# AdaLN-conditioned mixture-of-LoRA FFN: x's transposes and Bx regrouped over the tiles, the router's steps moved, Bx spread in fp32r

## The reference, cut to what matters

```python
# x (8, 512, 2048); cond_A, cond_B: 8 adapters of rank 16; base_w (2048, 2048), base_b (2048,)
# ffn A (64, 2048), ffn B (16 experts, 2048, 64), router_w (16, 2048)
def cond(x, A, B, ids):                      # one adapter per batch
    Bx = einsum('bni,bri->bnr', x, B[ids])
    return einsum('bnr,bor->bno', Bx, A[ids])
def ffn(y):
    base = einsum('bsi,oi->bso', y, base_w) + base_b
    hid = einsum('bsi,ri->bsr', y, A)
    probs = softmax(einsum('bsi,ei->bse', y, router_w))
    topw, topi = top_k(probs, 2);  topw /= sum(topw) + 1e-6
    combine = sum(one_hot(topi, 16) * topw)  # (b, s, 16)
    return base + 0.5 * einsum('bse,bsr,eor->bso', combine, hid, B)
out = x + ffn(cond(x, cond_A, cond_B, ids))
```

## Time and profile before

| | us |
|---|---|
| median of 3 runs (lowest, highest) | 446.38 (445.77, 449.51) |
| the profiled execution, its own time | 445.62 |
| its span, first to last instruction | 443.8 |
| PE busy in it | 409.7 (92%) |
| DVE busy | 319.4 (72%) |
| ACT busy | 108.1 (24%) |
| POOL busy | 40.5 (9%) |

### The profile page before, as it was taken

How to read it: one execution, slowest core, us unless ns; L and a number is a source line. 1 busy time by engine, 2 the same in 40 slices (tenths; PEclk the granted TensorE clock), 3 DMA queues, 4 the chain that set the end, 5 groups by cost and what they waited for, 6 DMA issues and landing times.

```text
span 443.8 us, 6785 instructions
## 1 busy us (share of the span) xinstructions
PE 409.7 (92%) x2496; PEld 279.9 (63%) x2496; DVE 319.4 (72%) x830; ACT 108.1 (24%) x163; POOL 40.5 (9%) x53
## 2 busy tenths in 40 slices
PE   0597997999788999999999999999999999999996
PEld 0475985656556766666667666666666676666665
DVE  2699996999468496668677875966686778756453
ACT  0003114435473231123113112311231131123110
POOL 4020000002100120012001201200120012012000
PEclk9999998999999999999999999999999999999999
DMA  8999999999999999899999999998999898556935
GB/s 223 357 330 331 334 357 366 345 269 336 289 295 239 352 362 323 279 349 342 310 287 378 306 315 302 366 312 295 348 335 325 285 366 303 207 201 217 343 128 189
DMA packets 75027, 135.35 MB, mean 305 GB/s; under 512 B 5506, under 2 KB 14770, under 8 KB 74994
## 3 DMA queue, kind: packets, MB, share of 16 engines
q1 hardware_dynamic: 56000, 102.08, 69.7%
q10 hardware_dynamic: 18994, 32.84, 23.5%
HBM read 99.23 MB, written 35.65 MB: 304 GB/s over the span
## 4 chain that ended last, share of the span: by engine, by line
PE 63%; DVE 10%; DMA 9%; SPq 6%; POOL 3%; ACT 3%; issue 3%; ACTq 2%; POOLq 0%; DVEq 0%
PE ps L927 13%; PE ps L928 11%; PE ps L929 11%; PE ps L901 11%; PE ps L941 6%; DMA bexpT<-in_x 6%; PE ps L930 5%; POOL u_r L480 3%; DMA gm_r<-xT 3%; DVE xT L728 3%; DVE early L659 3%; SPq L296 3%; ACT bexpT L495 2%; PE ps L856 2%; PE ps L949 2%
## 5 line engine op out<-in xcount | busy, mean ns | idle before, releaser
L840 DVE TENSOR_TENSOR xbuf<-ps,xbuf 128x512 f32<-128x512 f32 x128 | 86.7, 677 | 96.0 <-PE ps L930 96.0
L927 PE MATMUL ps<-h_r,u_r 128*128 128x512 f32 x256 | 108.8, 425 | 0.7
L928 PE MATMUL ps<-h_r,u_r 128*128 128x512 f32 x256 | 100.3, 392 | 0.0
L929 PE MATMUL ps<-h_r,u_r 128*128 128x512 f32 x256 | 100.1, 391 | 0.0
L866 PE MATMUL ps<-early 128*128 128x256 f32 x256 | 66.5, 408 | 22.6 <-DVE early L659 22.6
L728 DVE STREAM_TRANSPOSE xT<-xbuf 128x256 f32<-128x256 f32 x224 | 80.6, 410 | 0.0
L866 PEld LDWEIGHTS ps<-early 128*128 128x128 f32 x256 | 48.1, 201 | 36.8 <-issue 16.5
L927 PEld LDWEIGHTS ps<-h_r,u_r 128*128 128x128 f32 x256 | 48.1, 188 | 35.9 <-issue 16.7
L659 DVE STREAM_TRANSPOSE early<-xbuf 128x256 f32<-128x256 f32 x128 | 65.9, 577 | 5.3 <-issue 3.8
L901 PE MATMUL ps<-bexpT,cur 128*32 128x512 f32 x512 | 61.6, 598 | 2.2 <-DVE h_r L707 1.5
L495 ACT ACTIVATE h_r<-ps 128x512 fp32r<-128x512 f32 x64 | 36.2, 595 | 78.8 <-PE ps L901 78.4
(11 more groups left out here) (67 smaller groups left out, 205.3 us busy)
## 6 DMA issues: line engine op xcount, KB each, us to landing
out<-xbuf SPq DMA_DIRECT2D x31, 1024.0 KB, 7.3
xbuf<-in_x SPq DMA_DIRECT2D x28, 1024.0 KB, 7.4
xbuf<-in_x ACTq DMA_DIRECT2D x32, 512.0 KB, 10.9
xbuf<-in_x SPq DMA_DIRECT2D x32, 512.0 KB, 8.6
xbuf<-in_L_ffn_base_w SPq DMA_DIRECT2D x16, 512.0 KB, 19.3
xbuf<-in_L_ffn_base_w ACTq DMA_DIRECT2D x16, 512.0 KB, 20.1
gm_r<-g_hilo SPq DMA_DIRECT2D x128, 32.0 KB, 6.8
early_u<-in_L_ffn_B SPq DMA_DIRECT2D x10, 256.0 KB, 18.5
```

The costliest lines, as they stand in the source:

```text
L840: dve.tensor_tensor(xs, ps[:, tile_bank(b.n, m), :], xs, ALU.add).then_inc(s_out, 1)
L927: pe.matmul(acc, u_r[:, b.q, 0, h, tok_t], hi, start=(h == 0), stop=False)
L928: pe.matmul(acc, u_r[:, b.q, 0, h, tok_t], lo, start=False, stop=False)
L929: pe.matmul(acc, u_r[:, b.q, 1, h, tok_t], hi, start=False, stop=False)
```

## The change

x's transposes for a batch are now two per tile over 16 tiles, begun at tile 4 of two batches before and ended at tile 3 of the batch before (batches 0 and 1 have a schedule of their own). They stand behind the slot. Bx is computed in three groups (11, 11 and 10 products), each behind an h chunk: at tile 12 of the batch two before, and at tiles 0 and 4 of the batch before. The router's steps move: logits from 9 to 7, top 2 from 10 to 8, comb from 11 to 9, combk from 12 to 10, both flips from 13 and 14 to 11, u to 11. Batch 0 (for fronts 0 and 1) keeps its places except that the spread comes one slot after the logits and both flips are at 13. Bx is copied out once more in fp32r (`bxs_r`, high part by ACT, low part by DVE), and the spread is two fp32r products. The router's small tiles have their own memory, for which the DMA scratch is set to 1024 bytes. Refills of x move from tiles 4 and 8 (ACT) and chunks 0 and 1 (SP) to tiles 4 and 12.

```diff
-        spread = sb("spread", [P, 2, P])
+        spread = sb("spread", [P, 2, P], F32R)
+        bxs_r = sb("bxs_r", [P, 2, T], F32R)
+        router = sb("router", [P, 4, T])
-        sel = xT[:, 0, 0:NT * 2 * E]...       # comb, wt2, topf, topi, combk likewise
+        sel = router[:, 0, 0:NT * 2 * E]...
-        T_FIRST = {m: (2 * m, 2 * m + 1) for m in range(8)}
-        T_AHEAD = {12: (0,), 13: (1,), 14: (2,), 15: (3, 4)}
-        T_AT = {0: (5, 6), 1: (7,), 3: (8, 9), 4: (10, 11), 5: (12,), 6: (13, 14), 7: (15,)}
-        REFILL_AT = {4: 0, 8: 1}
-        def bx_before(f, m):
-            return {4 if f.n == 1 else 3: range(0, KD), 8: range(KD, 2 * KD)}.get(m, ())
+        LATE_AT = MT // 4
+        X_GROUPS = (11, 22)
+        def x_transposes(b, m):
+            if b == 0:
+                n, at = (1, 4 * m) if m < 8 else (2, 4 * (m - 10))
+                return [(n, at + i) for i in range(4) if 0 <= at < 2 * KD // n]
+            if b == 1 and m < 6:
+                return [(2, k) for k in range(KD + (0, 3, 6, 9, 12, 14)[m], KD + (3, 6, 9, 12, 14, 16)[m])]
+            if b == 1:
+                per, at = (2, 2 * (m - 6)) if m < 12 else (3, 12 + 3 * (m - 12))
+                return [(3, k) for k in range(at, at + per)]
+            if m < LATE_AT:
+                return [(b + 1, 2 * KD - 2 * LATE_AT + 2 * m + i) for i in range(2)]
+            return [(b + 2, 2 * (m - LATE_AT) + i) for i in range(2)]
+        def bx_groups(b, m):
+            a, e = X_GROUPS
+            if b == 0:
+                groups = {4: (1, (0, KD)), 8: (1, (KD, 2 * KD))}
+            elif b == 1:
+                groups = {0: (2, (0, KD)), 6: (2, (KD, 2 * KD)), 12: (3, (0, a))}
+            else:
+                groups = {0: (b + 1, (a, e)), 4: (b + 1, (e, 2 * KD)), 12: (b + 2, (0, a))}
+            return [groups[m]] if m in groups else []
+        def refills(b, m):
+            if b == 0:
+                return {4: [(2, 0)], 8: [(2, 1)]}.get(m, [])
+            if b == 1:
+                return {0: [(3, 0)], 8: [(3, 1)]}.get(m, [])
+            return {0: [(4, 0)] if b == 2 else [], 4: [(b + 2, 1)], 12: [(b + 3, 0)]}.get(m, [])
-        BXP_AT = 8
-        SPREAD_AT, MAX_AT, EXP_AT, TOP_AT, COMB_AT, COMBK_AT = 9, 9, 9, 10, 11, 12
-        CT_AT = UP_AT = {13: 0, 14: 1}
+        Steps = namedtuple("Steps", "bxp bx_lo logits peak exp spread top comb comb_k flips u")
+        FIRST_STEPS = Steps(8, 9, 9, 9, 9, 10, 10, 11, 12, 13, {13: (0,), 14: (1,)})
+        SECOND_STEPS = Steps(6, 6, 7, 7, 7, 7, 8, 9, 10, 11, {11: (0, 1)})
+        LATER_STEPS = Steps(4, 5, 7, 7, 7, 7, 8, 9, 10, 11, {11: (0, 1)})
...
 # ACT, slot: after the copy of Bx
+                    need(act, s_rep, f.n)
+                    copy(bxs_r[:, 0, :], ps[:, BXB, :]).then_inc(s_bxhi, 1)
 # DVE, slot
+                if m == at.bx_lo:
+                    dve.wait_ge(s_bxp, f.n + 1)
+                    dve.wait_ge(s_bxhi, f.n + 1)
+                    dve.tensor_tensor(bxs_r[:, 1, :], bxp, f32(bxs_r[:, 0, :]), ALU.subtract).then_inc(s_bxlo, 1)
 # DVE, step: the slot is behind the addition at every tile, and the transposes behind the slot
-                        if f is not None and m < MT - 1:
+                        if f is not None:
                             slot(f, m)
-                        if b.n + 2 < NB:
-                            for j in T_AHEAD.get(m, ()):
-                                x_transpose(Batch(b.n + 2), 2 * j)
-                                x_transpose(Batch(b.n + 2), 2 * j + 1)
+                        for n, k in present(x_transposes(b.n, m)):
+                            x_transpose(Batch(n), k)
 # PE, slot
-                    pe.matmul(ps[:, BXB, :], spread[:, f.q, :], bxp,
-                              start=True, stop=True).then_inc(s_rep, 1)
+                if m == at.spread:
+                    pe.wait_ge(s_bxhi, f.n + 1)
+                    pe.wait_ge(s_bxlo, f.n + 1)
+                    pe.matmul(ps[:, BXB, :], spread[:, f.q, :], bxs_r[:, 0, :], start=True, stop=False)
+                    pe.matmul(ps[:, BXB, :], spread[:, f.q, :], bxs_r[:, 1, :], start=False, stop=True)\
+                      .then_inc(s_rep, 1)
-                if m in CT_AT:
-                    h = CT_AT[m]
+                if m == at.flips:
                     pe.wait_ge(s_combk, f.n * 2 + 2)
+                    for h in range(2):                # both halves; half 1 waits for s_bx
...
+                        for n, span in present(bx_groups(b.n, c * NT + t)):
+                            bx_products(Batch(n), span)
                         tile_products(b, c, t)
...
-    nc = bacc.Bacc("TRN2", target_bir_lowering=False, num_devices=1)
+    nc = bacc.Bacc("TRN2", target_bir_lowering=False, num_devices=1, dynamic_dma_scratch_size=1024)
```

More of the change, by code:

```diff
@@ L23 @@
+from collections import namedtuple
 from contextlib import ExitStack
@@ L407, in step @@
                         continue
-                    if f is not None and c < 2 and not is_last(f):
-                        xquad_free(sp, f, c)
-                        load_xquad(sp, f.n + 1, c, range(0, NQ // 2))
+                    for n, g in present(refills(b.n, c * NT)):
+                        xquad_free(sp, n, g)
+                        load_xquad(sp, n, g, range(0, NQ // 2))
                     sp.wait_ge(s_out, b.n * MT + NT * (c + 1))
@@ L540, in h_hi, with slot @@
                     copy(h_r[:, c % 2, 0, h, :], ps[:, HB + h, :]).then_inc(s_hhi, 1)
[L542 to L546, removed]
+            def slot(f, m):
+                at = steps_of(f)
+                if m == at.bxp:
                     act.wait_ge(s_bxq, (f.n + 1) * 2 * KD)
@@ L591, in _ @@
                 if n in SLOT_AT:
-                    if SLOT_AT[n] in UP_AT:
+                    if SLOT_AT[n] in FIRST_STEPS.u:
                         act.wait_ge(s_gst[2], 16)
-                    slot(first, SLOT_AT[n], False)
+                    slot(first, SLOT_AT[n])
             act.wait_ge(s_wmm, NW)
@@ L610, in step @@
                             copy_experts(E_LATE[c * NT + t])
+                        for n, g in present(refills(b.n, c * NT + t)):
+                            xquad_free(act, n, g)
+                            load_xquad(act, n, g, range(NQ // 2, NQ))
                         if f is not None:
@@ L711, in x_transpose @@
                 g, j = k // KD, k % KD
-                place = ring_place(f, j)
                 cols = slice(j * SQ, (j + 1) * SQ)
@@ L722, in x_transpose, with slot @@
                         dve.wait_ge(s_xquad[g], f.n * NQ * 16)
-                if g == 0 and place == 0:
-                    need(dve, s_ct, f.n * 2)
                 if f.n < 2 and g == 0 and j in (KD // 2, 3 * KD // 4):
                     dve.wait_ge(s_ef, [e for e in range(GROUPS) if E_SLOT[e] == j // 4 + 1][f.n] + 1)
-                need(dve, s_bxq, f.n * 2 * KD + (0 if f.n == 2 and g == 0 else k - KD + 1))
-                dve.transpose(xh[:, place, :].rearrange("p (t l) -> p t l", l=SQ), src).then_inc(s_xe, 1)
-            def slot(f, m, x_too=True):
+                need(dve, s_bxq, f.n * 2 * KD + k - KD + 1)
+                dve.transpose(xh[:, j, :].rearrange("p (t l) -> p t l", l=SQ), src).then_inc(s_xe, 1)
+            def slot(f, m):
                 base = f.n * DVE_PER_FRONT
-                at = {MAX_AT: 0, TOP_AT: 1, COMB_AT: 10}.get(m, 0)
-                count = [at]
+                at = steps_of(f)
+                count = [{at.top: 1, at.comb: 10}.get(m, 0)]
                 def link(ins):
@@ L743, in wide @@
                     return ap.unsqueeze(2).to_broadcast([P, NT, E])
[L745 to L748, removed]
+                if m == at.bx_lo:
+                    dve.wait_ge(s_bxp, f.n + 1)
+                    dve.wait_ge(s_bxhi, f.n + 1)
+                    dve.tensor_tensor(bxs_r[:, 1, :], bxp, f32(bxs_r[:, 0, :]), ALU.subtract).then_inc(s_bxlo, 1)
+                if m == at.peak:
                     dve.wait_ge(s_lg, f.n + 1)
@@ L773, in slot @@
                                                   op0=ALU.add, op1=ALU.add))
-                if m == COMB_AT:
+                if m == at.comb:
                     after()
@@ L818, in _ @@
                 if n - SLOT_LAG in SLOT_AT:
-                    slot(first, SLOT_AT[n - SLOT_LAG], False)
+                    slot(first, SLOT_AT[n - SLOT_LAG])
             h_lo(first, 0)
@@ L931, in tile_products, with bx_products @@
                   .then_inc(s_acc, 1)
-            def bx_products(f, m):
-                for k in bx_before(f, m):
+            def bx_products(f, span):
+                for k in range(*span):
                     g, j = k // KD, k % KD
@@ L941, in bx_products @@
                     pe.matmul(ps[at:at + BK, BXB, g * (T // 2):(g + 1) * (T // 2)], bT[:, j, f.half, :],
-                              xh[:, ring_place(f, j), :], start=(j < NQ), stop=(j >= KD - NQ)).then_inc(s_bxq, 1)
```

(4 more changed lines are left out.)

55 lines of the change are left out of this document (26 added, 29 removed).

## The result

The changed kernel takes 482.86 us in the median (480.66 to 489.99), against 445.65 us for the kernel before measured beside it (445.35 to 449.51). The ratio is 1.080, 95% interval 1.075 to 1.085: 37 us slower. The forecast was 462, with a range of 453 to 469: the direction is right, but it gave 16 of the 37 us, and the measured time lies above the range. The profiled execution took 482.72, its span is 480.6.

The account below looks back on a forecast made before the run. PE was taken as the bound from the second batch on. Waits 18.4, less savings 7.9, plus first front 0.5, gave +11.0; clock falls +5.1; 445.62 became 461.7, put at 462 because the runs' median lay 0.8 higher. Range 453 to 469.

Parts of the forecast that it names:

- What bounds the kernel: From the second batch on, nothing is paid except through PE, busy 40.55 of a batch's 40.65 us.
- The savings, 1.3 a batch: PE work and waits removed in batches 2 to 5: 0.52 + 0.38 + 0.2 + 0.18 us; 7.9 in all batches.
- the group: Tile 3's Bx products, moved behind h chunks, take 1.72 us where they took 2.24: 0.52 saved a batch.
- the spread: Bx spread in the tiles' fp32r format: logits and spread save 0.38 us of PE a batch.
- the flips: Both flips of comb at one place, before an h chunk, take 0.78 us where they took 1.0: about 0.2 saved.
- the third cut of Bx: Cutting Bx into a third group costs nothing, as every group continues fp32 work.
- The wait at the flips: Behind tile 11, PE waits for comb: 3.1 us in batches 1 to 5, 2.4 in batch 6; none in batch 0.
- u sooner: PE's wait for the low half of u at the h chunk ending a batch goes: 0.18 us saved.
- The clock: Behind the new waits the clock falls to 1.2 GHz, 1.7 us each; 3 of 6 taken, +5.1 us.
- falls each time: Rival: the clock falls behind all six new waits, 10.2 us, total 468; chance 0.17.
- Part 7: Refills of x are asked for 8 tiles, about 19 us, ahead of the first transpose; nothing taken for them.
- x comes late: Rival: transposes wait for x, PE waits for Bx; 5 us in a few batches, total 470 to 480; chance 0.05.

Follow-up runs that it names:

- e8: Kernel before with the fp32r spread, the first Bx group behind an h chunk and both flips at tile 13, router and x unmoved: 439.89 us, ratio 0.986.
- e7: Kernel before with only Bx spread as two fp32r products one tile behind the logits, and the small DMA scratch: 444.33 us, ratio 0.996.
- the two doses: e4 and e5, which shorten DVE's chain to comb by 0.69 and 1.86 us against e1: 468.94 and 465.55 us.
- e5: e1 with no x transposes at tiles 8 to 10 and chunk 2's h halves made at tile 8, ahead of its result: 465.55 us, ratio 1.046.
- e10: e9 with all refills of x issued by ACT and none by SP: 453.82 us, ratio 1.017.
- e1: Changed kernel with batch 4's first-half refill of x issued at the end of batch 1: 475.05 us, ratio 1.063.
- e2: e1 with 12 unread products of 512 columns on PE ahead of the flips in fronts 2 to 7: 461.57 to 469.81 us, ratio 1.041.
- e4: e1 with x's two transposes of tile 8 done at tile 7: 468.94 us, ratio 1.053.
- e9: e5 with the flips behind tile 12's h chunk, the Bx group at tile 13 and batch 3's refill issued early: 461.34 us, ratio 1.034.
- e11: Changed kernel with ACT issuing all four quadrants of each refill of x and SP none: 471.94 us, ratio 1.056.

## Why the prediction was right or wrong, point by point

1. **What bounds the kernel**: right. Every gain and loss that was traced went through PE.
2. **The savings, 1.3 a batch**: a little high. e8 measures 40.65 - 39.61 = 1.04 a batch: about 0.49 for the group, 0.34 for the spread (e7), 0.17 for u, and only 0.06 for the flips, where 0.2 was counted. In the changed kernel one saving is eaten further: the third cut of Bx is not free, tile 3 to 4 takes 4.96 where 3.68 + 1.08 = 4.76 was counted.
3. **The wait at the flips, 3.1 in batches 1 to 5 and 2.4 in batch 6**: right in its place and its cause, which the two doses show. As idle time in the records it was to be 2.9; it is 2.94, 2.96 and 2.94 in batches 2 to 4, 3.77 in batch 1, 3.27 in batch 5, and 2.29 in batch 6.
4. **u sooner, and batch 0**: the wait for u at the start of a batch is gone, but in batch 1 a Bx group now stands at tile 0 and waits 0.76 for batch 0's u, which I had not looked for. The group at tile 6 of batch 1 waits for its last transposes too: tile 5 to 6 takes 4.74, where 1.59 + 2.25 = 3.84 was counted.
5. **The clock: a term that was mis-sized.** I took 3 falls of 6 at 1.7 each, 5.1. There were 5. With the wait taken off, tile 11 to 12 is 1.4 to 1.7 us longer in batches 1 to 4 than in e5 at full clock (6.0), and 2.9 longer in batch 5, where the clock stayed low for twice as long: 9.0 in all. The 3 of 6 was a choice between two bounds and no count. The case "falls each time" stood beside it with 0.17. The Trainium skill (TensorE: Matmul & The Clock Gate, section HAM oscillation) describes waits repeated in a loop that drop the clock each time. The trace agrees for batches 1 to 5, and not for batch 6.
6. **The refills: the step that failed.** Part 7 said that each quadrant group is asked for 8 tiles ahead, and took nothing for it. The diff has exceptions in plain sight: `{0: [(4, 0)] if b == 2 ...}` asks for batch 4's first half 4 tiles ahead, and batch 3's halves are asked for 6 and 5 tiles ahead. And SP reaches the refill for batch 4 8.7 us after the batch's first tile starts (225.2, against 216.5), since it stands at a reload until a store has landed; the data then takes 14.5 to land, 239.7 against a need at 228.8. With the lags that the prediction itself names, SP some 4 behind and a landing of 9.3 or at most 20.7, the same four tiles give 216.5 + 4 + 9.3 = 229.8 or 241, a wait of 1 to 12 us: not the 11, but a likely loss. The rival "x comes late" had the mechanism with 5 us at a chance of 0.05, and in its place it named the Bx groups at tile 12 or 4, where it was the spread at tile 7. "With a longer batch DMA gets easier" was wrong as well. From 150 to 400 us, first the kernel before, then the changed one, the DMA engines are busier and carry less, and SP's quadrants land after 14.6 us in the median in place of 8.6:

```profile
150.00:400.00 250.00, 249.28 (x1584) 162.85 (x1587) 182.59 (x524) 54.56 (x99) 25.50 (x25) 1.00 0.93 314
150.00:400.00 250.00, 223.53 (x1372) 145.55 (x1371) 166.26 (x476) 50.72 (x94) 23.85 (x24) 0.94 1.01 285
```

The sum: 11.0 of waits and savings as forecast, then from measured pieces 9.0 for the clock behind the flips, 11.0 for x in batch 2 (9.3 of wait and 1.6 of half clock behind it), 0.8 for the longer wait of batch 1 (DVE had waited 2.6 for x there), 0.9 and 0.8 for the two Bx groups of batch 1, 1.0 for tile 4's groups: 34.5 of the 36.8 between the last tiles' ends (476.86 against 440.09). Some 2 us are not assigned; the savings that came out lower, 0.3 a batch, are probably among them.

Still open: why the DMA engines are busier with fewer bytes in the changed order of transfers. That a batch is longer explains the lower GB/s (293 over batch 3 of the changed kernel, 332 over a batch of e8, nearly the same bytes), but not that the busy share is as high (1.01 and 1.00). The edits on SP's queue relieved the lateness but did not end it in e10. Open too is why some falls last twice as long.

## What to carry to other kernels

Moving a whole chain earlier by n tiles keeps its length only if the same work lies inside it and the same work covers it: here two moves of other work (transposes, h_lo) went into the chain and one cover (an h chunk) went out, and 0.9 of slack became 3.1 of wait. For each load whose request moves, count from the issuing queue's own place in its program, exceptions at the start of a stream first, not from the tile number in the schedule. On a PE that is otherwise never idle, a repeated wait of 2 us or more should be costed with the clock's fall behind it, 1.4 to 1.7 us each time in most cases here and 2.9 in some.

## What the runs showed of the hardware

These are counts over the traces of the changed kernel, e1, e2, e4, e5, e9, e10 and e11 of PE's waits of 1 us and more from batch 1 on. Behind waits of 2.9 us and more the granted clock fell to 0.50 each time (20 of 20, 15 of them at the flips of batches 1 to 5 in the changed kernel, e1 and e11). Behind waits of 1.96 to 2.55 it fell 9 times of 14: in batches 1 to 5 of e4, batch 4 of e5, batches 4 and 5 of e9 and batch 6 of e11. Behind waits of 1.1 to 1.6 it fell in none of 6. The length of the wait doesn't decide it alone: of the four waits of 2.3 at the flips of batch 6 (the changed kernel, e1, e4, e11) one was followed by a fall. A fall lasted 3.4 us at 1.2 GHz in 19 cases. Nine lasted 6.8 us, among them batch 5 of the changed kernel and of e1, batch 1 of e5 and of e11, and batches 4 and 5 of e9; the one at the late x in batch 2 of the changed kernel lasted 10.2, most of it while PE stood still. Filling a wait with 12 unread products kept the clock at 2.4 GHz in batches 2 to 4 and was worth 1.4 to 1.5 us a batch, although PE got to the flips no sooner.
